# Self-attention with a frequency convolution: half of the keys weighed from the kept scores of the maximum pass, turned by DMA

## What is computed

```python
# layer 0, for each of 4 images, n = m = 4096 points, 256 channels, 32 for q and k
q = Wq @ x; k = Wk @ x; v = Wv @ x
attn = softmax(q.T @ k / sqrt(32), axis=-1)        # 4096 x 4096
x = gamma * (Wo @ (v @ attn.T)) + x
# layer 1, in blocks of 8x8 points
low  = mean of each 2x2 square;  high = x - upsampled(low)
low  = prelu(bn(mag_w @ low + mag_b))
high = prelu(bn(phase_w @ concat([high, roll(high, 1, rows)]) + phase_b))[:256]
out  = upsampled(low) + high
```

## Time and profile before

| | us |
|---|---|
| median of 3 runs (2366.93 to 2368.57) | 2368.03 |
| the profiled execution | 2367.34 |
| its span | 2365.5 |

### The profile page before, as it was taken

One profiled execution on the slowest core, in us unless ns is written; L12 is line 12 of the kernel. 1 busy time (PEld: TensorE's weight loads), 2 busy tenths in 40 slices (PEclk: granted clock), 3 DMA queues, 4 the chain that ended last, 5 costly groups with the idle time before them and its releaser, 6 DMA issues.

```text
span 2365.5 us, 48520 instructions
## 1 busy us (share of the span) xinstructions
PE 2292.9 (97%) x16885; PEld 1843.7 (78%) x16885; DVE 1782.5 (75%) x2838; ACT 1369.4 (58%) x2547; POOL 720.5 (30%) x891
## 2 busy tenths in 40 slices
PE   5799999999989999999999999999999999999997
PEld 4587888887878887888877888888887777777786
DVE  6777787777777777887767877777887777778764
ACT  3365665565655656665546665656665555555564
POOL 3232332233232232332232332232332323133222
PEclk8899999999999999999999999999999999999998
DMA  4100111000110001111100000000000000000000
GB/s 166 56 29 30 40 40 40 31 21 28 40 41 32 31 27 31 40 40 32 35 22 24 31 31 31 21 10 31 31 31 22 22 12 9 21 21 21 21 18 19
DMA packets 42119, 75.50 MB, mean 32 GB/s; under 512 B 4864, under 2 KB 6144, under 8 KB 42080
## 3 DMA queue, kind: packets, MB, share of 16 engines
q1 hardware_dynamic: 42080, 75.00, 9.8%
HBM read 55.59 MB, written 19.40 MB: 32 GB/s over the span
## 4 chain that ended last, share of the span: by engine, by line
PE 91%; issue 3%; DVE 2%; POOL 1%; ACT 1%; DMA 0%; SPq 0%; DVEq 0%; ACTq 0%; POOLq 0%
PE O L521 19%; PE O L523 18%; PE O L522 18%; PE M L374 14%; PE M L411 10%; PE S L482 10%; PE M L392 1%; ACT p L641 1%; DVE pl L897 1%; PE M L417 1%; DMA uh<-in_x 0%; PE O L374 0%; DVE on L892 0%; POOL z L1051 0%; ACT ph L638 0%
## 5 line engine op out<-in xcount | busy, mean ns | idle before, releaser
L521 PE MATMUL O<-uh,ph 128*128 128x257 f16 x4096 | 1136.3, 277 | 2.3 <-DVE pl L897 1.9
L523 PE MATMUL O<-uh,pl 128*128 128x257 f16 x4096 | 1122.8, 274 | 0.0
L522 PE MATMUL O<-ul,ph 128*128 128x256 f16 x4096 | 1119.9, 273 | 0.0
L638 ACT ACTIVATE ph<-S 128x512 f16<-128x512 f32 x1024 | 612.6, 598 | 705.5 <-PE S L482 704.9
L805 DVE TENSOR_REDUCE pmax<-M 128x1 f32<-128x512 f32 (+1 forms) x1024 | 679.8, 686 | 329.2 <-PE M L411 317.4
L897 DVE TENSOR_TENSOR pl<-p,ph 128x512 f16<-128x512 f32 x1024 | 782.2, 765 | 136.6 <-ACT p L641 131.3
L641 ACT ACTIVATE p<-S 128x512 f32<-128x512 f32 x1024 | 609.5, 595 | 0.8
L521 PEld LDWEIGHTS O<-uh,ph 128*128 128x128 f16 x4096 | 401.0, 98 | 263.4 <-issue 142.3
L482 PE MATMUL S<-qcur,kst 128*128 128x512 f32 x1024 | 486.2, 479 | 21.6 <-ACT p L641 16.8
L523 PEld LDWEIGHTS O<-uh,pl 128*128 128x128 f16 x4096 | 402.0, 98 | 51.4
L522 PEld LDWEIGHTS O<-ul,ph 128*128 128x128 f16 x4096 | 405.1, 99 | 39.0
(11 more groups left out here) (147 smaller groups left out, 1697.6 us busy)
## 6 DMA issues: line engine op xcount, KB each, us to landing
xr<-in_x SPq DMA_DIRECT2D x37, 512.0 KB, 3.7
out_y<-z SPq DMA_DIRECT2D x32, 512.0 KB, 2.8
xb<-in_x SPq DMA_DIRECT2D x25, 512.0 KB, 3.6
xs<-in_x SPq DMA_DIRECT2D x21, 512.0 KB, 3.7
qraw<-q_scratch SPq DMA_DIRECT2D x99, 64.0 KB, 1.9
ul<-in_x SPq DMA_DIRECT2D x4, 512.0 KB, 7.6
uh<-in_x SPq DMA_DIRECT2D x4, 512.0 KB, 8.3
q_scratch<-qsave SPq DMA_DIRECT2D x32, 64.0 KB, 1.6
```

Of the source, the lines that this page charges most:

```text
L521: nc.tensor.matmul(O[j][:, 0:UW], ph[:, t % 4, q], uh[parity][:, t, :], start=(t == 0), stop=False)
L522: nc.tensor.matmul(O[j][:, 0:C], ph[:, t % 4, q], ul[parity][:, t, :], start=False, stop=False)
L523: ins = nc.tensor.matmul(O[j][:, 0:UW], pl[:, t % 4, q], uh[parity][:, t, :], start=False, stop=(t == MT - 1))
L638: nc.scalar.activation(ph[:, t % 4, :], S[t % 2][:, :], ACT.Exp, scale=SCALE)
```

## The change

The keys of an image are split in two halves. For the first (chunks 0 to 3, 16 tiles) everything stays. For the second (chunks 4 to 7, `TURNED`) the scores that the maximum pass computes are kept: `saved_max` writes the bank to `saved` (16 slots of 128 queries x 512 keys in fp32) and takes the maximum in the same VectorE instruction. One turn later ScalarE exponentiates a slot with the negated maximum as bias, once to fp16 and once to fp32, VectorE subtracts the low part, a DMA transpose (128 x 1024 fp16) from SyncE's queue turns both parts into `pt`, a ring of four, and `weigh_slot` adds them: twelve matmuls, all into one O[j]. The 32 steps are now UNITS: six tiles, then slot and tile in turn ten times, then six slots. A slot's exponentials stand five steps ahead of it, its low part four. There are 16 `scores` a turn where there were 32. The maxima of the kept half come last and in the slots' order; `DOUBLE` is new, and negmax of a FULL turn stands at step 30 instead of 29.

To make room, `uh` and `ul` are held for one image only. The next image's go through `uh_next` and `ul_next` to device memory, chunk by chunk, and come back in the last turn of an image, each part once its last reader is done. The buffers xs, on, qsave, nhi, pair and low4 share memory with others; the output store is issued one turn later than before, and the scan reads xr. The diff's core (SP is SyncE, pe TensorE, act ScalarE, dve VectorE):

```diff
-DOUBLE = (8, 10, 14, 16, 18, 22, 24, 26)
-MAXIMA = [(j, m) for j in range(SUB) for m in range(NCH)]
+DOUBLE = (7, 8, 10, 12, 14, 16, 18)
+ND, NK = MT // 2, MT // 2
+TURNED = range(NCH // 2, NCH)
+RING = 4
+RISE = 6
+UNITS = [("d", i) for i in range(RISE)]
+for i in range(ND - RISE):
+    UNITS += [("k", i), ("d", RISE + i)]
+UNITS += [("k", k) for k in range(ND - RISE, NK)]
+AT = {unit: t for t, unit in enumerate(UNITS)}
+EXP_AHEAD, LOW_AHEAD = 5, 4
...
+MAXIMA = [(j, m) for j in range(SUB) for m in range(NCH) if m not in TURNED] + [(j, m) for m in TURNED for j in range(SUB)]
+def slot_of(j, m):
+    return (m - TURNED[0]) * SUB + j
...
+                              first=3, doubled=(6, 8, 10, 12, 14, 16, 18)),
...
+        saved = sb("saved", [128, NK, CH])
+        pq = sb("pq", [128, RING, 2, CH], f16)
+        pt = sb("pt", [128, RING, 2 * SUB, 128], f16)
...
+            def turn_slot(g, k):
+                sp.wait_ge(slot_low, NK * g + k + 1)
+                sp.wait_ge(k_weighed, NK * g + k + 1)
+                sp.sem_inc(turn_seen, 1)
+                sp.dma_start_transpose(pt[:, k % RING, :, :], pq[:, k % RING, :, :].rearrange("p v n -> p (v n)"))\
+                    .then_inc(turned[k % RING], 16)
...
+            def load_u(m, filled):
+                sp.dma_start(uh_flat[:, m * SUB * UW:(m + 1) * SUB * UW], uh_dram[m]).then_inc(filled, 16)
+                sp.dma_start(ul_flat[:, m * SUB * C:(m + 1) * SUB * C], ul_dram[m]).then_inc(filled, 16)
+            def load_direct_u(g, m):
+                sp.wait_ge(d_weighed, ND * g + SUB * (m + 1))
+                load_u(m, u_direct_loaded)
+            def load_turned_u(g, m):
+                sp.wait_ge(k_weighed, NK * g + slot_of(SUB - 1, m) + 1 + RING)
+                load_u(m, u_turned_loaded)
...
+                turn_slot(g, 0)
                 if plan is not FINAL:
...
+                    fetch_q((c + 2) % NCH if isinstance(c, int) else ds((c + 2) % NCH, 1))
+                turn_slot(g, 1)
+                if plan is FULL:
+                    emptied(sp, plan, g, ("u", 1))
+                    sp.dma_start(flat(uh_dram), uh_next_flat[:, :]).then_inc(u_stored, 16)
+                    sp.dma_start(flat(ul_dram), ul_next_flat[:, :]).then_inc(u_stored, 16)
+                sp.wait_ge(out_ready, g + 1)
+                gp = (g + (ALL - 2)) % ALL
+                sp.dma_start(out_v[ds(gp // NCH, 1), ds(gp % NCH, 1)], z[:, :, :]).then_inc(out_stored, 16)
+                turn_slot(g, 2)
...
+                if ends_image:
+                    sp.wait_ge(u_stored, 32 * g + 64)
+                    sp.sem_inc(turn_seen, 1)
+                    load_direct_u(g, 0)
+                turn_slot(g, 3)
...
-                sp.dma_start(xr[:, :, :], x_v[ds(g // NCH, 1), ds(g % NCH, 1)]).then_inc(xr_loaded, 16)
                 if scans:
+                    gs = (g + 2 * NCH) % ALL
+                    sp.dma_start(xr[:, :, :], x_v[ds(gs // NCH, 1), ds(gs % NCH, 1)]).then_inc(xs_loaded, 16)
+                else:
+                    sp.dma_start(xr[:, :, :], x_v[ds(g // NCH, 1), ds(g % NCH, 1)]).then_inc(xr_loaded, 16)
+                turn_slot(g, 4)
+                if ends_image:
+                    load_direct_u(g, 1)
+                turn_slot(g, 5)
+                turn_slot(g, 6)
+                if ends_image:
+                    load_turned_u(g, TURNED[0])
+                turn_slot(g, 7)
...
-                sp.wait_ge(out_ready, g + 2)
-                gp = (g + (ALL - 1)) % ALL
-                sp.dma_start(out_v[ds(gp // NCH, 1), ds(gp % NCH, 1)], z[:, :, :]).then_inc(out_stored, 16)
-            turns(sp, turn)
+                    sp.dma_start(xr[:, :, :], x_v[ds(g // NCH, 1), ds(g % NCH, 1)]).then_inc(xr_loaded, 16)
+                turn_slot(g, 8)
...
+                if i == 0:
+                    pe.wait_ge(u_direct_loaded, 128 * (g // NCH) + 16)
+                pe.wait_ge(lo_ready, ND * g + i + 1)
...
+            def weigh_slot(g, k):
+                if k == 0:
+                    pe.wait_ge(u_turned_loaded, 128 * (g // NCH) + 16)
+                pe.wait_ge(turned[k % RING], 16 * (NK // RING * g + k // RING + 2))
+                j, ends = k % SUB, k >= NK - SUB
+                for i in range(SUB):
+                    t = SUB * TURNED[k // SUB] + i
+                    nc.tensor.matmul(O[j][:, 0:UW], pt[:, k % RING, i, :], uh[:, t, :], start=False, stop=False)
+                    nc.tensor.matmul(O[j][:, 0:C], pt[:, k % RING, i, :], ul[:, t, :], start=False, stop=False)
+                    ins = nc.tensor.matmul(O[j][:, 0:UW], pt[:, k % RING, SUB + i, :], uh[:, t, :],
+                                           start=False, stop=(ends and i == SUB - 1))
+                ins.then_inc(k_weighed, 1)
...
+                    if kind == "d" and i + LEAD < ND:
+                        scores(g, parity, i + LEAD)
...
-                        pe.wait_ge(probs_ready, MT * g + MT - 1)
-                        scores(g + 1, parity, 0)
-                        pe.wait_ge(lo_ready, MT * g + MT)
-                        scores(g + 1, parity, 1)
-                    weigh(g, parity, t)
+                        pe.wait_ge(probs_ready, ND * g + ND)
+                        for n in range(LEAD):
+                            scores(g + 1, parity, n)
...
+                act.wait_ge(k_weighed, NK * g + RING - SUB + j + 1)
+                act.wait_ge(high_ready, g + 1)
...
+            def slot_probabilities(g, k):
+                if k == 0:
+                    act.wait_ge(bias_ready, g + 1)
+                act.wait_ge(turned[k % RING], 16 * (NK // RING * g + k // RING + 1))
+                bias = nbias[:, k % SUB:k % SUB + 1]
+                nc.scalar.activation(pq[:, k % RING, 0, :], saved[:, k, :], ACT.Exp, scale=SCALE, bias=bias)
+                nc.scalar.activation(saved[:, k, :], saved[:, k, :], ACT.Exp, scale=SCALE, bias=bias).then_inc(slot_probs, 1)
...
-                for t in range(MT):
-                    if 0 < t < MT - LEAD:
-                        probabilities(g, t + LEAD)
+                for t, (unit, i) in enumerate(UNITS):
+                    if t > 0 and unit == "d" and i + LEAD < ND:
+                        probabilities(g, i + LEAD)
+                    for k in slots_at(t, EXP_AHEAD):
+                        slot_probabilities(g, k)
...
+            def saved_max(bank, j, m, free):
+                nc.vector.tensor_scalar(saved[:, slot_of(j, m), :], bank[:, :], 0.0, None, ALU.add, ALU.max,
+                                        accum_out=pmax[:, j, m:m + 1]).then_inc(free, 1)
...
+                dve.wait_ge(nmax_ready, count)
+                nc.vector.tensor_scalar(nbias[:, :], nmax[:, :], SCALE, None, ALU.mult).then_inc(bias_ready, 1)
...
-                    if t + 1 < MT:
-                        low_probabilities(g, t + 1)
+                    if t + 1 < MT and UNITS[t + 1][0] == "d":
+                        low_probabilities(g, UNITS[t + 1][1])
+                    for k in slots_at(t, LOW_AHEAD):
+                        slot_low_probabilities(g, k)
...
-                        partial_max(bank, task[1], task[2], free)
+                        if task[2] in TURNED:
+                            dve.wait_ge(slot_low, NK * g + slot_of(*task[1:]) + 1)
+                            saved_max(bank, task[1], task[2], free)
+                        else:
+                            partial_max(bank, task[1], task[2], free)
...
                         dve.wait_ge(xs_loaded, (g + 1) * 16)
-                        scan(amax[:, parity, ds(c, 1)], xs[:, :, :], xs_scanned)
+                        scan(amax[:, parity, ds(c, 1)], xr[:, :, :], xs_scanned)
```

More of the change, by code:

```diff
@@ L45, with slots_at @@
 ROUND_X, ROUND_CONV, SCAN, NEGATIVE = 9, 14, 12, 26
-DOUBLE = (8, 10, 14, 16, 18, 22, 24, 26)
-MAXIMA = [(j, m) for j in range(SUB) for m in range(NCH)]
+DOUBLE = (7, 8, 10, 12, 14, 16, 18)
[9 more added lines that the diff above has]
+EXP_AHEAD, LOW_AHEAD = 5, 4
+def slots_at(t, ahead):
+    return [k for k in range(NK) if AT["k", k] - ahead == t]
+MAXIMA = [(j, m) for j in range(SUB) for m in range(NCH) if m not in TURNED] + [(j, m) for m in TURNED for j in range(SUB)]
+def slot_of(j, m):
+    return (m - TURNED[0]) * SUB + j
 class Plan:
@@ L72, in steps_with_maxima @@
         for _ in range(2 if t in doubled else 1):
-            steps.setdefault(t, []).append(("max",) + left.pop(0))
+            j, m = left.pop(0)
+            assert m not in TURNED or t >= AT["k", slot_of(j, m)] - LOW_AHEAD
+            steps.setdefault(t, []).append(("max", j, m))
         t += 1
@@ L83 @@
 LAST = Plan(steps_with_maxima({4: [("y", 0)], 5: [("y", 1)], 19: [("low", 0, 1)], 21: [("high", 0)], 23: [("high", 1)]},
-                              first=3, doubled=(6, 8, 10, 12, 14, 16, 18, 24, 25)),
+                              first=3, doubled=(6, 8, 10, 12, 14, 16, 18)),
             before=(FULL, ALL - NCH))
@@ L145, in attention_conv @@
```

(54 more changed lines are left out.)

185 lines of the change are left out of this document (102 added, 83 removed).

## The result

The changed kernel takes 2341.4 us (median of 4 runs, 2340.3 to 2342.9), the kernel before beside it 2368.3: the ratio is 0.989 (95% interval 0.987 to 0.990). The forecast was 2278. The direction is right and 2341 lies in the range, but of the 90 us forecast only 27 came. The 512 scores went as said, and of the 123 us that they were worth, 96 were given back where 34 were forecast.

A forecast was written before the change was run, and what follows sets the result against it. TensorE, busy 97% of the span, was taken as the bound. 2367.3 less 123 for scores gives 2244; plus 33 VectorE, 3 staged values, 3 LAST-turn stretch, less 5 turn ends, makes 2278 us; range 2238 to 2440.

The forecast's parts named there:

- 512 scores: TensorE: 16 of 32 score matmuls go in each of 32 turns, 0.24 us each, 123 us gained.
- VectorE, steps 7 to 18 of FULL turns: VectorE needs 22.4 us, 23.1 with the scan, against TensorE's 21.9; a turn loses 0.9 or 1.6, together 33 us.
- LAST turns, turn ends and stretch: Eight last turns: 5 us gained from a removed wait at turn ends, 3 us lost in the VectorE stretch.
- values staged: Next image's values through device memory: two stores a turn, eight 256 KB loads at three image ends; 3 us lost.
- transposes, SyncE's queue: 512 DMA transposes hidden, costing nothing: latency to landing L = 3 us, spacing R = 1.5 us; SyncE's queue also nothing.
- The case that was given 0.24: Rival 1: transposes set the pace; at a spacing of 5.6 us the kernel takes 2996 us; chance 0.24.
- Nothing, up to 0.3 a turn: ScalarE: exponentials keep their number, half read SBUF at 0.04 us more at most; costs nothing, up to 0.3 us a turn.
- The slots have two to three steps of slack: ScalarE, steps 0 to 6: 8 tile pairs, 3 slots and copies against TensorE's 17.3 us; slots have slack to spare.
- bunching: VectorE, steps 7 to 18: two low parts before the maxima of every even step, none in odd ones; 0.4 us added.
- The accumulator: VectorE: reductions that also write 512 scores to SBUF take 0.1 us more each, 0.6 us in steps 7 to 18.
- Rival 2: VectorE takes the gain: kept low parts last 1.04 instead of 0.75 us, 86 us more, 2364 us; chance 0.10.
- near nothing: Sign: VectorE's idle time in steps 7 to 18 near nothing, with TensorE's waits there on the kept maxima.

The follow-up runs named there:

- e1_exp6: Changed kernel with the kept slots' exponentials six steps ahead of their weighing instead of five, low parts as they were: 2309.4 us, ratio 0.976.
- e4_no_bias: Changed kernel with the slots' exponentials without bias operand and at a quarter of the scale (output not the reference's): 2318.1 us, ratio 0.979.
- e9_low_first: Changed kernel with ScalarE normalising the low convolution ahead of the slot's exponentials in steps 19 and 20, not behind them: 2323.3 us, ratio 0.982.
- e10_double24: As e8_scan22, with the second maximum of step 8 moved to step 24 in FULL turns: 2264.8 us, ratio 0.956.
- e8_scan22: Changed kernel with slot exponentials six steps ahead (slots 0 and 1 five) and the scan moved from step 12 to 22: 2277.1 us, ratio 0.962.

## Why the prediction was right or wrong

Term by term, in us over all turns:

| term | forecast | measured |
|---|---|---|
| 512 scores | -123 | -123 |
| VectorE, steps 7 to 18 of FULL turns (all their loss, 86, less the next row) | +33 | +61 |
| steps 5 and 20 of FULL turns (ScalarE's queue) | 0 | +25 |
| LAST turns, turn ends and stretch | -2 | +10 |
| values staged | +3 | 0 |
| transposes, SyncE's queue | 0 | 0 |

The rows go by place and not by cause: e1_exp6, which moves only exponentials on ScalarE, took most of the stalls at steps 9 and 17 away too.

**The scores** held. A plain slot step is 1.32 and one with a maximum 1.57, so the first maximum costs 0.25 also where no score stands beside it. The last turn, which has no maxima, is the clean case: its first 31 steps took 56.77 us before and take 52.99 now, 3.78 less where 3.84 was forecast.

**The transposes** held. R was taken at 1.5 and L at 3. Measured: 3.1 us to landing (3.0 to 5.5), and the median transpose holds SyncE's queue for 1.233 us; the weighing waited three times for one, 0.9 us together. The case that was given 0.24 did not come.
**The step that failed is ScalarE's,** "Nothing, up to 0.3 a turn", and with it the sum made for VectorE. Three things were wrong in it.
1. The slack was counted to the wrong reader. "The slots have two to three steps of slack" is the time until a slot is weighed. But its first reader is VectorE's queue, one step behind ScalarE's place (five ahead against four), and everything behind the low part waits with it. e1_exp6 moves only this distance, for 32 us.
2. Size. It said at most 0.04 us for an exponential from SBUF, from a copy without a bias (634 ns in the earlier trace rows). That row was right for the source (628 ns in e4_no_bias) and blind to the bias: 721. The trace of before had rows that show it (groups by line of the kernel before: an activation of 128x512 with one column operand, and with two, where the plain one of L638 has 598 ns):

```profile
L664 ACT ACTIVATE z<-M,bnB,bnA 128x512 f32<-128x512 f32 x66 | 51.3, 778 | 118.2 <-PE M L374 118.2
...
L651 ACT ACTIVATE uh<-M,uscale 128x512 f32 x48 | 33.2, 691 | 9.2 <-PE M L374 8.6
```

   691 - 598 = 93 and 778 - 691 = 87 ns for a column; 721 - 628 = 93 was measured. The Trainium skill has the rule (ScalarE: Activation LUTs, What ACT_TABLE_LOAD costs): each per-partition pointer operand, scale or bias, adds about 93 ns. The trace agrees. The prediction used neither.
3. ScalarE also empties a bank, for the low convolution at step 20. The slot's exponentials, a pair of 1.22 us, were put in front of it, and the question "what is queued behind the new instruction" was not asked there: 18 us by e9_low_first.

**VectorE's stretch** had the right place and the right kind of wait, and a wrong mechanism. The prediction compared sums, 22.4 of work against 21.9 of TensorE, and called the rest "bunching", 0.4. But a sum bounds a stretch only from below. VectorE measured 21.3 busy, less than reckoned, and still 2 to 3 us were lost. TensorE is ahead of VectorE by two banks M at most, so one operation of 1.2 us behind a late one is enough. The scan shows it: reckoned as 0.7 a turn of missing time, it cost 15.6 / 16 = 1.0, nearly its full length. The "bunching" of low parts beside GpSimd is seen at step 17, as 0.60. The accumulator, for which 0.1 was added, costs no more than that: its reading instruction is 82 ns, and the next operation starts 0.61 to 0.68 us after a kept maximum, against 0.60 for the plain one.

**Rival 2,** "VectorE takes the gain", came nearer in its number (2364) than the forecast, for another reason than it gave. Low parts of a slot last 741 ns on average, where it had supposed 1.04 us. The long ones do harm where one is late already (step 17), not by their sum. What the list of signs said of VectorE's idle time ("near nothing") was the sign that failed: it was 2.6 us a stretch, and read at once it would have told the order from the amount.

**Staged values and turn ends.** The turns that bring an image's values back are as long as their neighbours (70.67 and 70.67), so the 3 us were none. An image end has sixteen loads of some 256 KB, not the eight of the prediction (24 of `uh` and 24 of `ul` at three ends); its 4 MB are those of sixteen. Of the 5 us at the turn ends no run speaks alone: LAST turns lost 1.4 each in the change. In e10_double24 most have 63.57, 0.2 under 67.60 - 3.84, so something was gained there, less than 0.6 each as far as seen.

The forecast, 2278, is nearly what e8_scan22 takes, the change with its exponentials and its scan in other places. That isn't to its credit; it means that the sum of work allowed 2278 and the order did not.

## What to carry to other kernels

When work is added to an in-order queue, don't compare sums of busy time: list what stands behind the new instruction on its engine, and take its lateness as theirs; slack counts to the first queue that waits, not to the last use. An engine that is waited for and is idle in the same window asks for another order first; here one number (how many steps ahead) was worth 32 us, and four edits of order 77. And price an instruction by its position: the same 0.09 us an exponential was worth 23 us in one order and nothing in another.

## What the runs showed of the hardware

- A DMA transpose of 128x1024 fp16 from SBUF to SBUF lands 3.1 us after its issue and holds its queue 1.233 us; the same bytes as a plain copy land in 2.3. It makes some 910 packets more than the copy ((596576 - 129632) / 512), and they slowed no engine that these traces show.
- An exponential of 128x512 on ScalarE takes 602 ns from PSUM, 628 from SBUF, and 721 from SBUF with a bias column.
- A maximum with the scores kept costs VectorE 0.61 to 0.68 us from start to start (1491.16 to 1491.77 above), hardly more than the maximum alone, though the accumulator's reading appears as an instruction of 82 ns.
- A low part on VectorE, which reads two operands in SBUF, takes 0.60 us or up to 1.19 to the next start while GpSimd works, and the average of 741 ns hides both; the maxima, which read PSUM, stay at 0.60 to 0.63 in the same stretch (482.87 above: three in 1.88, with the next start at 484.75). In the whole trace of the change the 822 low parts that no GpSimd instruction overlaps last 0.68 to 0.70 us, and no maximum lasts longer than that, whatever GpSimd does.
- The low part is held until the GpSimd instruction that was running has ended, and then takes its time: of the 369 low parts of the kernel before that started while a GpSimd instruction ran, 344 end 0.54 to 0.56 us after the end of that instruction, and in the change 151 of 169. In the others the instruction had at most 0.06 us left; they take their usual 0.68 to 0.70, but for five that last 1.22 to 1.27, with the next GpSimd instruction behind it. Where the low part is first, GpSimd's instruction is the longer one (1.27 against 0.72 us above). The Trainium skill says this of the two (SBUF — State Buffer, Who interferes with whom): a VectorE instruction with two inputs in SBUF contends with a GpSimd instruction that reads SBUF, a reduction never does, and the contention is an exclusive lock. The trace agrees, with these durations; no run here took GpSimd away.
